# A sparse graph layer on one core: whole 8 KB runs of the matrix, x and out in blocks of four tiles, and new orders of work on three engines

## The chip, the cores and the metric

One core of one Trainium2 chip. The metric is the device time of one execution in microseconds (us); the program runs alone. The core has five engines that run their own instruction streams and meet at semaphores: TensorE (PE), VectorE (DVE), ScalarE (ACT), GpSimd (POOL) and SyncE (SP). SP issues the plain transfers and GpSimd the indirect ones (gathers), each into its own DMA queue; 16 DMA engines serve both.

## The reference

x is 8192 × 512 and adj 8192 × 8192, both in float32. Few entries of adj are positive: about nine in a row, the one on the diagonal always among them. The layer is

```python
h = jnp.maximum(_layernorm(x, axis=-1), 0.0)
mask = adj > 0
head = mask.astype(adj.dtype)
head = head / jnp.maximum(jnp.sqrt(jnp.sum(head * head, axis=-1, keepdims=True)), 1e-12)
inc = adj + head
out = x + (inc @ h) / jnp.sum(inc, axis=-1, keepdims=True)
```

so each positive entry of a row gets a constant added (one over the root of their number), and the product is divided by the row's sum.

## The kernel before, in words

The matrix is not multiplied: its positive entries are found, the rows of h that they name are gathered, and small products add them up.

**Stage 1** (up to about 80 us) reads x in 16 blocks of 1 MB, computes h and stores it in DRAM (`h_scratch`). In a block c, partition p holds the four adjacent rows 512c + 4p + j. The first four blocks (16 tiles of x) stay in SBUF (`held`, x_held).

**Stage 2** runs over 64 tiles of 128 rows. Tile t is c = t // 4, j = t % 4: partition p holds row 512c + 4p + j. SP loads a tile's 4 MB into one of two buffers `A[:, t % 2]` in four chunks of 1 MB (`load_chunk`, L378). Chunk j holds columns 1024j and on of the left half and the same columns of the right half, two runs of 4 KB in each partition:

```python
adj_h = adj.rearrange("(c p j) (h n) -> c j p h n", p=P, j=ROWS, h=2)
sp.dma_start(chunk(t % 2, j), adj_h[t // ROWS, t % ROWS, :, :, CW * j:CW * (j + 1)])
```

VectorE folds the two halves of a chunk into one word per column pair (`fold`, L774), takes the eight largest of each chunk (MAX8, L779) and their places (FIND_INDEX8, L783). That is up to 32 candidates a row, of which 8 are the "own" ones of each row; what is left over goes to "spill" places that rows of a tile share, in three groups of 128. Between the folds VectorE does the small steps of earlier tiles: weights (L914), ranks of the spilled entries (L859) and, after they were brought to their places by TensorE, their entries (L941, own_entry). Tiles 62 and 63 are "wide": unfolded, searched in eight parts (L797, L802), with four spill groups. Rows for which the fold lost an entry go, up to 128 of them, through one extra "batch" tile, number 64, gathered row by row. A dense path for more such rows stands at the end and has no rows here.

The engines are staggered. In period t VectorE searches tile t, and with p = t−1, q = t−2, r = t−3, f = t−4 the others do, each in an order written out by hand:

- **TensorE** (`period`, L1361): find_owner(q), product_spill(f) (L1341, 3 products of 128×128 by 128×512), residual(q) (L1318 adds x, then L1323 adds the row's own h by a diagonal), offsets(p) (L1278), bring_spill(q) (L1301 writes pbrought, L1307 pturned), product_own(q) (L1330, eight products with diagonals). A product leaves two records in the profile. product_spill(f) ends tile f and releases acc_ready.
- **ScalarE** (`period`, L669): check 0 of tile t, own_matrices(q) (L632, nine diagonals), row_again(q) (L642, h of the tile's own rows from x), spill_columns(r) and spill_matrix(r) (L615, L623), roots(p) (L585), copy_owner(q) (L607), checks 1 and 2, finish_tile(f) (L649, copies the sum out of PSUM, waits for acc_ready), reach_places(p) (L593 to L600), check 3. The checks (L569) read the whole tile once more and count its zeros, to find rows that the fold can't take. The buffer of a chunk is loaded again when the fold and the check have read it.
- **GpSimd** (loop at L514): gather_spill(t−2), 3 gathers of 128 rows of h, then gather_own(t), 8 gathers (L488).
- **SP** (loop at L412): chunks 0 and 1 of tile t+2, the store of out of tile t−4 (`store_tile`, L394, from one of two buffers osb, named out_tile), the load of x of tile t from tile 16 on (`load_x`, L387, into one of two buffers xres, named x_residual), chunks 2 and 3 of tile t+2. x and out move 256 KB at a time, 2 KB in a row.

`batch_period` (L701 on ScalarE, L1383 on TensorE) and `drain` (L1399) end the staggered work.

## Time and profile before

| | |
|---|---|
| Runs of the kernel before | 1261.79, 1264.53, 1265.77 us; median 1264.53 |
| The profiled execution's own time | 1265.03 us |
| Its span (first to last instruction) | 1263.2 us |
| VectorE busy | 1162.8 us (92%) |
| ScalarE busy | 977.8 us (77%) |
| TensorE busy | 970.4 us (77%), mean granted clock 0.908 |
| GpSimd busy | 764.9 us (61%) |
| DMA | 471.29 MB, mean 373 GB/s |

How to read it: the busy time of an engine is that of its instructions, without the waits between them; TensorE's products are pipelined, so that its busy share does not mean that each product runs at its peak. In a timeline a line is one instruction or a run of adjacent ones of one kind, with the time that it starts, the time it takes, and in brackets how long its engine idled before it and which event ended that.

### The profile page before, as it was taken

To read this page: it belongs to the slowest core of one execution; us is meant where nothing else is said; L and a number is where in the kernel's file an instruction comes from. 1 tells how busy PE (TensorE), PEld (TensorE's weight loads), DVE (VectorE), ACT (ScalarE), POOL (GpSimd) and SP (SyncE) were. 2 spreads that over 40 slices of the span, in tenths; PEclk is the share of its full clock that TensorE was granted. 3 is DMA by queue.
4 is the path that set the end of the run, shared out by engine and by line. 5 is a ranking of instruction groups with operands and counts; after the bars stand their busy time and mean duration, and the time that the engine had idled before them with its cause. 6 is when DMAs were issued, how large, how long until landed. Compare 5 with 4: busy or idle time off the path is not lost.

```text
span 1263.2 us, 14630 instructions
## 1 busy us (share of the span) xinstructions
PE 970.4 (77%) x2678; PEld 482.8 (38%) x2678; DVE 1162.8 (92%) x2794; ACT 977.8 (77%) x1903; POOL 764.9 (61%) x745
## 2 busy tenths in 40 slices
PE   0002889988888888888888888798888878878676
PEld 0001334444444434444433444344444434434343
DVE  6679999999999999999998999989999989998972
ACT  6657888898888887888887787788878778876551
POOL 1003666766666667676666666775666667667453
PEclk9999999888889999889988988988899889998698
DMA  9999999999999999999999999999999999999442
GB/s 360 428 421 406 398 402 392 392 394 399 396 391 402 401 399 398 384 401 394 384 398 368 400 398 391 388 395 373 402 400 400 385 382 387 398 399 355 142 143 79
DMA packets 148127, 471.29 MB, mean 373 GB/s; under 512 B 24386, under 2 KB 24386, under 8 KB 143876
## 3 DMA queue, kind: packets, MB, share of 16 engines
q1 hardware_dynamic: 90368, 331.38, 66.9%
q0 software_dynamic: 57664, 138.93, 29.9%
q8 instruction: 25, 0.41, 0.1%
q14 instruction: 70, 0.57, 0.1%
HBM read 490.21 MB, written 33.82 MB: 415 GB/s over the span
## 4 chain that ended last, share of the span: by engine, by line
DVE 45%; DMA 20%; issue 20%; ACT 5%; SPq 5%; another core or an unknown queue 2%; PE 1%; DVEq 0%; ACTq 0%; POOL 0%; POOLq 0%
DMA adj_tile<-in_adj_dram 17%; DVE folded L774 15%; DVE cand_word L779 12%; DVE cand_index L783 5%; DMA gathered_rows<-in_x_dram 3%; SPq L385 2%; ACT junk L569 2%; DVE cand_word L797 2%; SPq L392 2%; DVE cand_index L802 2%; ACT adj_tile L556 2%; SPq L396 1%; DVE ln_stats L757 1%; DVE weights_and_payload L914 1%
## 5 line engine op out<-in xcount | busy, mean ns | idle before, releaser
L488 POOL DMA_INDIRECT gathered_rows<-h_scratch,slot_column x520 | 536.8, 1032 | 265.9 <-issue 161.2
L569 ACT ACTIVATE junk<-adj_tile,zero_unit 128x2048 bf16<-128x2048 f32 x256 | 510.1, 1994 | 111.2 <-issue 75.5
L1330 PE MATMUL acc<-gathered_rows,diag 128*128 128x512 f32 x1040 | 504.1, 641 | 0.5 <-issue 0.5
L488 POOL DMA_INDIRECT gathered_rows<-h_scratch,spill_column x197 | 220.5, 1119 | 199.0 <-ACT spill_column L615 150.8
L774 DVE SCALAR_TENSOR_TENSOR folded<-adj_tile 128x1024 f32<-128x1024 f32 x248 | 301.4, 1215 | 12.1 <-DMA adj_tile<-in_adj_dram 10.7
L1330 PEld LDWEIGHTS acc<-gathered_rows,diag 128*128 128x128 f32 x1040 | 213.7, 212 | 247.1 <-issue 246.8
L779 DVE MAX8 cand_word<-folded 128x8 f32<-128x1024 f32 x248 | 302.9, 1221 | 2.2
L783 DVE FIND_INDEX8 cand_index<-cand_word,folded 128x8 uint32<-128x1024 f32 x248 | 302.2, 1218 | 0.0
L1341 PE MATMUL acc<-gathered_rows,spill_matrix 128*128 128x512 f32 x394 | 186.3, 607 | 14.6 <-issue 10.7
L632 ACT ACTIVATE diag<-ident,weights_and_payload 128x128 f32<-128x128 f32 x582 | 176.2, 387 | 0.5 <-DVE weights_and_payload L914 0.5
L1278 PE MATMUL poff<-spill_rank,lanes_before 128*128 128x1 f32 x130 | 26.4, 272 | 187.5 <-DVE spill_rank L859 174.4
L1278 PEld LDWEIGHTS poff<-spill_rank,lanes_before 128*128 128x128 f32 x130 | 25.4, 227 | 239.8 <-issue 139.7
L1341 PEld LDWEIGHTS acc<-gathered_rows,spill_matrix 128*128 128x128 f32 x394 | 73.9, 194 | 103.0 <-issue 102.9
L1323 PE MATMUL acc<-own_row,diag 128*128 128x512 f32 x124 | 75.2, 691 | 45.4 <-ACT own_row L642 29.2
L1307 PE MATMUL pturned<-ident,owner 128*128 128x128 f32 x394 | 79.2, 355 | 0.0
L1301 PE MATMUL pbrought<-weights_and_payload,owner 128*128 128x72 f32 (+1 forms) x386 | 71.4, 333 | 3.5 <-ACT owner L607 3.3
L1307 PEld LDWEIGHTS pturned<-ident,owner 128*128 128x128 f32 x394 | 68.8, 257 | 0.0
L615 ACT ACTIVATE spill_column<-entry 128x3 uint32<-128x3 f32 (+1 forms) x65 | 12.8, 198 | 72.3 <-issue 44.1
L1318 PE MATMUL acc<-x_residual,ident 128*128 128x512 f32 x96 | 53.2, 637 | 17.9 <-issue 14.3
L1301 PEld LDWEIGHTS pbrought<-weights_and_payload,owner 128*128 128x128 f32 x386 | 62.5, 239 | 5.9 <-ACT owner L607 4.5
L623 ACT ACTIVATE spill_matrix<-pturned,entry 128x128 f32<-128x128 f32 x197 | 56.6, 356 | 3.9 <-remote 3.9
L1323 PEld LDWEIGHTS acc<-own_row,diag 128*128 128x128 f32 x124 | 23.1, 211 | 88.1 <-ACT diag L632 46.0
(146 smaller groups left out, 829.8 us busy)
## 6 DMA issues: line engine op xcount, KB each, us to landing
adj_tile<-in_adj_dram SPq DMA_DIRECT2D x256, 1024.0 KB
h_scratch<-adj_tile SPq DMA_DIRECT2D x16, 1024.0 KB, 10.5
out_dram<-out_tile SPq DMA_DIRECT2D x64, 256.0 KB
gathered_rows<-in_x_dram SPq DMA_DIRECT2D x12, 1024.0 KB, 12.6
x_residual<-in_x_dram SPq DMA_DIRECT2D x48, 256.0 KB
gathered_rows<-h_scratch,slot_column POOLq DMA_INDIRECT x520
x_held<-in_x_dram SPq DMA_DIRECT2D x4, 1024.0 KB, 7.9
gathered_rows<-h_scratch,spill_column POOLq DMA_INDIRECT x197
```

The costliest lines, as they stand in the source:

```text
L488: nc.gpsimd.indirect_dma_start(out=into, out_offset=None, in_=h[:, :], in_offset=bass.IndirectOffsetOnAxis(ap=column, axis=0), bounds_chec ...
L569: nc.scalar.activation(junk[:, n % 2].rearrange("p (j c) -> p j c", j=2), both[:, :, half], ACT.Relu, bias=zero_unit[:], scale=-UP, accum_ ...
L623: last = nc.scalar.activation(W[:, t % 2, g], pturned[:, g * P:(g + 1) * P], ACT.Copy, scale=entry[:, t % 2, g, 0:1])
L632: last = nc.scalar.activation(diag[:, t % 2, s], ident[:], ACT.Copy, scale=wpay[:, t % 2, s:s + 1])
L774: nc.vector.scalar_tensor_tensor(out=F[:, j % 2], in0=a[:, 1], scalar=UP, in1=a[:, 0], op0=ALU.mult, op1=ALU.add).then_inc(folded, 1)
L779: nc.vector.max(out=cv[:, t % 2, 8 * j:8 * j + 8], in_=F[:, j % 2]).then_inc(vals_found, 1)
L783: nc.vector.max_index(out=ci[:, t % 2, 8 * j:8 * j + 8], in_max=cv[:, t % 2, 8 * j:8 * j + 8], in_values=F[:, j % 2]).then_inc(idx_found, 1)
L1301: last = nc.tensor.matmul(bank[:, c:c + 3 * n], owner[:, g * P:(g + 1) * P], wpay[:, t % 2, 1 + OWN:1 + OWN + 3 * n], start=True, stop=True)
L1307: last = nc.tensor.matmul(pturned[:, g * P:(g + 1) * P], owner[:, g * P:(g + 1) * P], ident[:], start=True, stop=True)
L1323: nc.tensor.matmul(acc[t % 3][:], diag[:, t % 2, 0], again[:], start=False, stop=False).then_inc(row_added, 1)
L1330: last = nc.tensor.matmul(acc[t % 3][:], diag[:, t % 2, 1 + s], slot(t % 2, s), start=False, stop=False)
L1341: last = nc.tensor.matmul(acc[t % 3][:], W[:, t % 2, g], slot(t % 2, OWN + g), start=False, stop=(g == groups(t) - 1))
```

## The change

Four things change together.

1. **Runs of the matrix.** A chunk is 2048 adjacent columns, one run of 8 KB in each partition. The fold joins the chunk's own two halves, so columns n and n + 1024 instead of n and n + 4096; constants of columns, the place of the diagonal and the numbering of the wide tiles' parts follow.
2. **x and out.** Five blocks of x (20 tiles) are held instead of four; out of a tile is written by finish_tile over its x in the same place. SP stores out in 16 blocks of 1 MB (8 KB runs) and loads the other 11 blocks of x as 1 MB where a block has been stored. The small buffers and the semaphore res_added go away; finish_tile no longer waits for a store.
3. **Orders.** GpSimd gathers own rows of tile t ahead of the spill rows of t−2; the gather of x for the batch tile goes behind the loop. TensorE does residual and product_own first, then offsets, bring_spill, and product_spill(f) last. ScalarE does row_again(q) and own_matrices(q) ahead of check 0, moves roots behind check 1, and does finish_tile(f) last, behind check 3.
4. **Batch tile.** It gets four spill groups like the wide tiles, and one VectorE step of the final marking goes away.

The diff, cut to its core:

```diff
-    HELD_CHUNKS = 4
+    HELD_CHUNKS = 5
...
-    x_t = x.rearrange("(c p j) d -> c j p d", p=P, j=ROWS)
-    out_t = out.rearrange("(c p j) d -> c j p d", p=P, j=ROWS)
-    adj_h = adj.rearrange("(c p j) (h n) -> c j p h n", p=P, j=ROWS, h=2)
+    out_ln = out.rearrange("(c p j) d -> c p j d", p=P, j=ROWS)
+    adj_t = adj.rearrange("(c p j) n -> c j p n", p=P, j=ROWS)
...
-            return EXTRA if FOLDED <= t < BATCH else FOLDED_EXTRA
+            return EXTRA if wide(t) else FOLDED_EXTRA
...
-                sp.dma_start(chunk(t % 2, j), adj_h[t // ROWS, t % ROWS, :, :, CW * j:CW * (j + 1)]).then_inc(adj_loaded[t % 2][j], 16)
-
-            def load_x(t):
-                if t >= HELD + 2:
-                    sp.wait_ge(res_added, t - 1)
-                    if not wide(t - 2):
-                        sp.wait_ge(row_ready, t - 1)
-                sp.dma_start(xres[:, t % 2], x_t[t // ROWS, t % ROWS]).then_inc(x_loaded[t % 2], 16)
-
-            def store_tile(t):
-                sp.wait_ge(out_ready, t + 1)
-                sp.dma_start(out_t[t // ROWS, t % ROWS], osb[:, t % 2]).then_inc(out_stored[t % 2], 16)
+                sp.dma_start(A[:, t % 2, 2 * CW * j:2 * CW * (j + 1)],
+                             adj_t[t // ROWS, t % ROWS, :, 2 * CW * j:2 * CW * (j + 1)]).then_inc(adj_loaded[t % 2][j], 16)
+
+            def load_x(c):
+                sp.wait_ge(out_stored[(c - HELD_CHUNKS) % 2], 16 * ((c - HELD_CHUNKS) // 2 + 1))
+                sp.dma_start(group(c), x_ln[c]).then_inc(x_loaded[c % 2], 16)
+
+            def store_group(c):
+                sp.wait_ge(out_ready, ROWS * c + ROWS)
+                sp.dma_start(out_ln[c], group(c)).then_inc(out_stored[c % 2], 16)
...
-                if t >= 4:
-                    store_tile(t - 4)
-                if t >= HELD:
-                    load_x(t)
+                if t >= 2 * ROWS and t % ROWS == 0:
+                    store_group(t // ROWS - 2)
+                if t % ROWS == 2 and HELD_CHUNKS <= t // ROWS - 2 + HELD_CHUNKS < LN:
+                    load_x(t // ROWS - 2 + HELD_CHUNKS)
...
-                gather_spill(t - 2)
-                if t < BATCH:
-                    gather_own(t)
+                gather_own(t)
+                if t >= 2:
+                    gather_spill(t - 2)
...
             def finish_tile(t):
                 act.wait_ge(acc_ready, t + 1)
-                if t >= 2:
-                    act.wait_ge(out_stored[t % 2], 16 * (t // 2))
-                nc.scalar.activation(osb[:, t % 2], acc[t % 3][:], ACT.Copy).then_inc(out_ready, 1)
+                nc.scalar.activation(out_of(t), acc[t % 3][:], ACT.Copy).then_inc(out_ready, 1)
...
-                check(t, 0)
                 if pay:
-                    own_matrices(q)
                     if not wide(q):
                         row_again(q)
+                    own_matrices(q)
...
+                check(t, 0)
                 if pick:
                     spill_columns(r)
                     spill_matrix(r)
-                if small:
-                    roots(p)
                 if pay:
                     copy_owner(q)
                 check(t, 1)
+                if small:
+                    roots(p)
                 check(t, 2)
-                if end:
-                    finish_tile(f)
                 if small:
                     reach_places(p)
                 check(t, 3)
+                if end:
+                    finish_tile(f)
...
                 if pay:
                     find_owner(q)
-                if end:
-                    product_spill(f)
...
                 if pay:
                     residual(q)
+                    product_own(q, 0)
+                    product_own(q, 1)
                 offsets(p)
                 if pay:
                     bring_spill(q)
-                    product_own(q, 0)
-                if pay:
-                    product_own(q, 1)
+                if end:
+                    product_spill(f)
...
                 step(nc.vector.scalar_tensor_tensor(out=w_well[:, 6], in0=end_all[:, last],
                                                     scalar=float(PLACES), in1=w_well[:, 5], op0=ALU.is_le, op1=ALU.add))
-                step(nc.vector.scalar_tensor_tensor(out=w_well[:, 6, TILES - FOLDED:], in0=end_all[:, BATCH:BATCH + 1],
...
```

In `batch_period` the same two moves are made: on TensorE product_spill(u) goes behind product_own of the next tile but two, on ScalarE finish_tile(u) goes behind the first check of the batch tile.

## Rows read from the trace of the kernel before

**Rows 1.** The page: busy time of the engines, DMA share in 40 slices, gather queue.

```profile
PE 970.4 (77%) x2678; PEld 482.8 (38%) x2678; DVE 1162.8 (92%) x2794; ACT 977.8 (77%) x1903; POOL 764.9 (61%) x745
...
DMA  9999999999999999999999999999999999999442
...
q0 software_dynamic: 57664, 138.93, 29.9%
```

**Rows 2.** Windows: stretch, length, PE, PEld, DVE, ACT, POOL busy, PEclk, DMA share, GB/s.

```profile
150.00:430.00 280.00, 244.08 (x690) 123.34 (x689) 277.98 (x652) 236.60 (x465) 190.81 (x185) 0.91 1.02 396
430.00:1126.00 696.00, 596.85 (x1645) 294.52 (x1644) 665.93 (x1561) 568.51 (x1119) 471.18 (x441) 0.91 1.02 392
```

**Rows 3.** VectorE's timeline: the first fold of tiles 1, 36, 37 and 61.

```profile
97.81 1.22 DVE L774 SCALAR_TENSOR_TENSOR folded<-adj_tile 128x1024 f32<-128x1024 f32 x1 [1.18 <-DMA adj_tile<-in_adj_dram]
...
692.87 1.22 DVE L774 SCALAR_TENSOR_TENSOR folded<-adj_tile 128x1024 f32<-128x1024 f32 x1
...
709.56 1.22 DVE L774 SCALAR_TENSOR_TENSOR folded<-adj_tile 128x1024 f32<-128x1024 f32 x1
...
1126.32 1.21 DVE L774 SCALAR_TENSOR_TENSOR folded<-adj_tile 128x1024 f32<-128x1024 f32 x1
```

**Rows 4.** DMA view, 31.6 to 50 us, then 90 to 105 us: packets, MB, share.

```profile
q1 hardware_dynamic: 1086, 7.86, 101.0%
...
q1 hardware_dynamic: 1497, 6.26, 102.4%
```

**Rows 5.** ScalarE's timeline around 661, 693 and 705 us.

```profile
661.25 0.80 ACT L642 ACTIVATE own_row<-x_residual,ln_bias,ln_rstd 128x512 f32<-128x512 f32 x1
661.96 0.19 ACT L615 ACTIVATE spill_column<-entry 128x3 uint32<-128x3 f32 x1
...
693.36 2.73 ACT L632 ACTIVATE diag<-ident,weights_and_payload 128x128 f32<-128x128 f32 x9
...
704.89 0.57 ACT L649 ACTIVATE out_tile<-acc 128x512 f32<-128x512 f32 x1
705.37 0.16 ACT L593 ACTIVATE half_minus_offset<-poff 128x1 f32<-128x1 f32 x1
```

**Rows 6.** TensorE's timeline around 664, 702 and 1251 us.

```profile
663.98 1.02 PE L1323 MATMUL acc<-own_row,diag 128*128 128x512 f32 x2
664.84 0.28 PE L1278 MATMUL poff<-spill_rank,lanes_before 128*128 128x1 f32 x2
...
666.40 7.03 PE L1330 MATMUL acc<-gathered_rows,diag 128*128 128x512 f32 x16
...
701.62 0.38 PE L1278 MATMUL poff<-spill_rank,lanes_before 128*128 128x1 f32 x2 [1.85 <-DVE spill_rank L859]
701.86 0.87 PE L1301 MATMUL pbrought<-weights_and_payload,owner 128*128 128x72 f32 x6
...
703.28 8.73 PE L1330 MATMUL acc<-gathered_rows,diag 128*128 128x512 f32 x16
...
1251.11 2.74 PE L1341 MATMUL acc<-gathered_rows,spill_matrix 128*128 128x512 f32 x6
```

**Rows 7.** Windows: the stretches around these own products, columns as in rows 2.

```profile
660.00:674.00 14.00, 13.79 (x45) 6.89 (x44) 13.40 (x31) 9.44 (x21) 10.82 (x11) 1.00 1.03 399
703.30:706.70 3.40, 3.40 (x7) 1.34 (x6) 3.37 (x5) 3.40 (x7) 2.65 (x3) 0.50 1.03 400
```

**Rows 8.** VectorE's timeline: own_entry, then the first searches of both wide tiles.

```profile
712.47 0.22 DVE L941 TENSOR_TENSOR own_entry<-pbrought,place_plus_half 128x72 f32<-128x72 f32 x1
...
1143.68 1.22 DVE L797 MAX8 cand_word<-adj_tile 128x8 f32<-128x1024 f32 x1
...
1169.48 1.21 DVE L797 MAX8 cand_word<-adj_tile 128x8 f32<-128x1024 f32 x1
```

**Rows 9.** DMA view, 263 to 268 us: both queues, packets, MB, share.

```profile
q1 hardware_dynamic: 338, 1.15, 59.3%
q0 software_dynamic: 291, 0.80, 41.9%
```

More of the change, by code:

```diff
@@ L190, in x_of, with group, out_of, x_come @@
         def x_of(t):
-            return held[:, t] if t < HELD else xres[:, t % 2]
-        def x_turn(t):
-            return (t - HELD) // 2 + 1
+            return held[:, t % HELD]
+        def group(c):
+            k = c % HELD_CHUNKS
+            return held[:, ROWS * k:ROWS * (k + 1), :]
+        def out_of(t):
+            return again[:] if t == BATCH else held[:, t % HELD]
+        def x_come(t):
+            c = t // ROWS
+            return x_loaded[c % 2], 16 * ((c - HELD_CHUNKS) // 2 + 1)
         incT = F[:, 0, 0:2 * P].rearrange("p (b c) -> p b c", b=2)
@@ L242, in searched @@
             return CHUNKS * min(t, FOLDED) + PARTS * max(t - FOLDED, 0)
-        def part(i):
-            return i % 2 * CHUNKS + i // 2
         def paid(t, k):
@@ L422, in _ @@
                     load_chunk(t + 2, 3)
-            for t in range(TILES - 4, TILES):
-                store_tile(t)
+            for c in range(LN - 2, LN):
+                store_group(c)
             for b in range(2):
-                sp.wait_ge(out_stored[b], 16 * (TILES // 2))
+                sp.wait_ge(out_stored[b], 16 * (LN // 2))
             sp.wait_ge(list_ready, 1)
@@ L434, in _ @@
                     sp.dma_start(A[:, 0, :], adj[bass.ds(row, P, step=ROWS), :]).then_inc(d_adj, 16)
-                    sp.dma_start(xres[:, 0], x[bass.ds(row, P, step=ROWS), :]).then_inc(d_x, 16)
+                    sp.dma_start(held[:, 0], x[bass.ds(row, P, step=ROWS), :]).then_inc(d_x, 16)
                     for c in range(NCH):
@@ L440, in _ @@
                     sp.wait_ge(d_out, j + 1)
-                    sp.dma_start(out[bass.ds(row, P, step=ROWS), :], osb[:, 0]).then_inc(d_stored, 16)
+                    sp.dma_start(out[bass.ds(row, P, step=ROWS), :], held[:, 1]).then_inc(d_stored, 16)
                     sp.wait_ge(d_stored, j * 16 + 16)
@@ L511, in _ @@
                 pool.wait_ge(h_stored[b], 16 * (LN // 4))
-            gather_own(0)
-            gather_own(1)
-            for t in range(2, BATCH + 1):
+            for t in range(BATCH - 1):
                 if t == BATCH - 2:
@@ L704, in batch_period @@
                 own_matrices(w)
-                finish_tile(u)
                 check_batch(0)
@@ L708, in batch_period @@
                 reach_places(y)
+                finish_tile(u)
                 check_batch(1)
@@ L786, in part_columns @@
             def part_columns(t, i):
-                if t == BATCH:
-                    return A[:, 0, CW * part(i):CW * (part(i) + 1)]
-                return chunk(t % 2, part(i) % CHUNKS)[:, part(i) // CHUNKS]
+                return A[:, t % 2, CW * i:CW * (i + 1)]
             def part_values(t, i):
@@ L794, in part_values @@
                 else:
-                    dve.wait_ge(adj_loaded[t % 2][part(i) % CHUNKS], 16 * turn(t))
-                e = slice(8 * part(i), 8 * part(i) + 8)
+                    dve.wait_ge(adj_loaded[t % 2][i // 2], 16 * turn(t))
+                e = slice(8 * i, 8 * i + 8)
                 nc.vector.max(out=cv[:, t % 2, e], in_=part_columns(t, i)).then_inc(vals_found, 1)
@@ L800, in part_places @@
                 dve.wait_ge(vals_found, searched(t) + i + 1)
-                e = slice(8 * part(i), 8 * part(i) + 8)
+                e = slice(8 * i, 8 * i + 8)
                 nc.vector.max_index(out=ci[:, t % 2, e], in_max=cv[:, t % 2, e],
@@ L1316, in residual @@
                 elif t >= HELD:
-                    pe.wait_ge(x_loaded[t % 2], 16 * x_turn(t))
-                nc.tensor.matmul(acc[t % 3][:], ident[:], again[:] if t == BATCH else x_of(t), start=True,
-                                 stop=False).then_inc(res_added, 1)
+                    pe.wait_ge(*x_come(t))
+                nc.tensor.matmul(acc[t % 3][:], ident[:], again[:] if t == BATCH else x_of(t), start=True, stop=False)
                 if not wide(t):
@@ L1385, in batch_period @@
                 find_owner(w)
-                product_spill(u)
                 residual(w)
@@ L1391, in batch_period @@
                 product_own(w, 1)
+                product_spill(u)
                 find_owner(y)
```

41 lines of the change are left out of this document (19 added, 22 removed).

## The prediction

> **What bounds the kernel now.** I read the page first. Its busy line and slices [rows 1] show VectorE busy for 92% of the span, TensorE for 77%, and the DMA engines full until the last three slices. Two limits thus lie close together, and the windows by stage [rows 2] separate them only a little: from 150 to 430 us VectorE is busy 277.98 of 280 us, from 430 to 1126 us 665.93 of 696, while the DMA share is 1.02 in both. The starts of the first fold of a tile [rows 3] give the pitch: (1126.32 − 97.81)/60 = 17.14 us a tile, where an undelayed tile takes 709.56 − 692.87 = 16.69. So the loop costs 60 × 0.45 = 27 us over what VectorE needs. The other side of the same number is the traffic: 16.69 us at 392 GB/s move 6.54 MB, and a tile needs 4.19 MB of the matrix, 138.93/65 = 2.14 MB of gathered rows [rows 1] and 0.46 MB of x and out, 6.79 MB or 17.3 us. VectorE is the floor at 16.7 and the DMA engines hold the loop 0.4 above it. ScalarE and TensorE have slack, and this change spends it.
>
> **The change part by part.**
>
> *Matrix in 8 KB runs.* Before, a chunk is two 4 KB runs a partition. No row shows 8 KB runs of the matrix, but the loads of x at the start are 8 KB runs with nothing beside them, and 90 to 105 us is almost only matrix [rows 4]: 7.86 MB in 18.4 us, 427 GB/s, against 6.26 MB in 15.0 us, 417. 64 tiles of 4.19 MB are 268.4 MB: 643.6 − 628.6 = 15 us less DMA time. The bounds are 0 (the two stretches differ in direction too, since the first holds stores of h) and, with the shares of 102.4% and 101.0% counted in, 268.4 × (1.024 × 15.0/6.26 − 1.01 × 18.4/7.86) = 24 us. I take 15, the time that passed.
>
> *x and out in blocks.* 48 + 64 transfers of 256 KB in 2 KB runs become 11 + 16 of 1 MB in 8 KB runs: 29.4 MB. The gathers are 2 KB rows; their queue moved 138.93 MB in 29.9% of 1263.2 us [rows 1], 368 GB/s. At that rate 29.4 MB take 79.9 us, at 427 GB/s 68.9: 11 us less. Bounds 0 and, if stores lose as much again by short runs, 22. SP issues fewer transfers, and load_x and store_group stand where load_x and store_tile stood, ahead of chunks 2 and 3 of tile t+2. The store at turn t waits for out_ready of tile t−5, finished at the end of period t−1, the load for a store issued two turns before; I cost both waits at nothing, because a 1 MB transfer takes some 3 us at 400 GB/s and they have two turns of 17 us. Without that cover each late one would hold two chunks back, once in four tiles. The sum of both DMA parts is 26 us, 0.41 a tile of 64: 17.14 becomes 16.73, no longer above VectorE's 16.69.
>
> *The orders of TensorE and ScalarE.* Here the path changes. Before, product_spill(f) is second in TensorE's period and finish_tile(f) comes after check 2 on ScalarE: it never waits in the loop, and the diagonals and the row of tile q lie between checks. After, product_spill(f) is the last of TensorE's period, finish_tile(f) is ScalarE's last and waits for it, and the next period's row_again and nine diagonals stand behind it; TensorE's row product and own products wait for those diagonals, and offsets, bring_spill and product_spill stand behind them. That closes a ring of one turn per tile through both engines, worked out from ScalarE's rows [rows 5] and TensorE's rows at full clock [rows 6]:
> - finish_tile until the next instruction: 705.37 − 704.89 = 0.48.
> - row_again 661.96 − 661.25 = 0.71, nine diagonals 2.73.
> - the row product 664.84 − 663.98 = 0.86.
> - the eight own products 7.03 (16 records).
> - offsets, pbrought and pturned: 666.40 − 664.84 = 1.56.
> - product_spill 2.74 for three groups.
>
> This is 16.11; with the handovers between the engines I take 16.2 us. What else ScalarE does (checks, spill_matrix, copy_owner, roots, reach_places) lies beside TensorE's 12.2 us: its busy 568.51 of 696 us [rows 2] are 14.0 a tile, less 3.9 in the ring 10.1. Against 16.7 the ring would be just hidden, if TensorE stayed at full clock.
>
> *The clock.* In each turn TensorE has nothing but find_owner and the residual to do while ScalarE does 0.48 + 0.71 + 2.73 = 3.92 us: it idles about 3 us (3.92 less one product of 0.86). Before, a wait of 1.85 us ahead of offsets [rows 6] was followed by a stretch at granted clock 0.50, the 1.2 GHz level [rows 7], and the own products took 8.73 us there, against 7.03 in the stretch at 1.00: 1.70 us lost. The new idle is longer and stands straight ahead of the same products. With one such stretch a turn the ring takes 16.2 + 1.7 = 17.9 us. The lower bound is the loop's own mean clock, 0.91 [rows 2]: TensorE's 12.19 us become 13.4, and the ring 17.4. The upper bound is a second such stretch in a third of the turns, 17.9 + 0.57 = 18.5. I take 17.9, since the row with the idle ahead is nearest to what the ring makes.
>
> *What of it the end sees.* 60 × (17.9 − 17.14) = +45.6. Some of the lag is hidden. own_entry on VectorE starts at 712.47 [rows 8], 9.7 us after pbrought came (701.86 + 0.87) [rows 6]; bringing it behind the own products uses about 7 of these and leaves some 3 at the beginning of the loop. At the end the wide tiles take VectorE 1169.48 − 1143.68 = 25.8 us each [rows 8], so that a ring of 17.9 regains perhaps half of 7.9. Together −7, an estimate (bounds 0 and −12).
>
> *Small parts.* GpSimd issues the own gathers of t ahead of the spill gathers of t−2: own rows come three issues earlier, spill rows eight later, and by the code both are used a period or more after their issue; nothing on the path. The gather of x for the batch tile stands behind the loop, ahead of tile 61's spill gathers, and is used later still: nothing. The batch tile gets a fourth group: a third of 2.74 on TensorE, 0.9, and about 0.5 for one more matrix and gather: +1.4, an estimate, in the tail, where nothing covers it; the marking step removed on VectorE is within its rounding. finish_tile loses its wait for a store and TensorE its release of x, both met long before; nothing. The last store is 1 MB in place of 256 KB: 0 to +4 us, but it lies beside the batch tile's work (product_spill of its predecessor ends at 1253.85 [rows 6]): 0.
>
> **Sum** against the profiled execution's 1265.0: +45.6 − 7 + 1.4 = +40, thus 1305; the median of the runs shown is 0.5 lower, 1304.5. The DMA relief does not appear in it, since the ring, not the transfers, sets the pitch. Its own range is 1275 (17.4) to 1339 (18.5).
>
> **Rivals.**
> - *The ring stays hidden (faster).* TensorE keeps its clock, as in the stretch at 1.00 [rows 7], and the pitch falls to 16.73: 60 × −0.41 + 1.4 = −23, 1241. For it: 16.2 is below 16.7 at full clock, and the DMA engines do lose 26 us of work. Against it: the clock was 0.91 with less idle than the ring makes, and the ring has 0.5 us to lose. It decides where less than 0.5 us of TensorE's clock is lost per turn.
> - *The two cancel (same).* Half of the turns have such a stretch: 16.2 + 0.85 = 17.05; 60 × −0.09 + 1.4 = −4, 1260.5; with a little more of it 1268.
> - *Gathers starve (slower).* In 5 us with both queues busy [rows 9] the loads send 338 packets of 140 ns and the gathers 291 of 115 ns: nearly turn by turn. With the loads' packets twice as long the gathers' share falls from 0.41 to 115/395 = 0.29, and their 5.8 us a tile (29.9% of 1263.2 over 65) take 20 us instead of 14. They would then set 20 us for as long as loads always queue; as loads stop when both buffers are full, I count between a sixth and a half of the excess of 2.9 over 17.14: 60 × 0.5 = +30 to 60 × 1.4 = +85, 1294 to 1350, about 1323 for a third. For it: packets do grow with the runs (1086 for 7.86 MB of 8 KB runs, 1497 for 6.26 MB of 4 KB runs) [rows 4]. Against it: the rows' lead of a period. The Trainium skill, "DMA: Bandwidth & Descriptors", section "Queues, rings and completion order", states the rule behind this: an engine takes turns between the queues at packet granularity. The near equality of 338 and 291 agrees with it; by it alone the longer packet takes time from the gathers.
> - *8 KB runs are no faster.* Then DMA still needs 17.14, and with the ring hidden the time is that of before.
>
> **How the numbers follow.** The forecast 0.56, starved gathers 0.08, cancelling or no faster packets 0.12, hidden ring 0.24. A measurement of this kernel tells 0.3%, 3.8 us, from no change. Slower is 0.56 + 0.08, the same 0.12, faster 0.24. The range reaches from the hidden ring's own centre, 1241, which leaves out half of it (0.12), to 1340, which leaves out the worst of starving and of the clock (0.08).
>
> **What would show it.** Right: ScalarE's finish_tile waits for product_spill in most tiles, by a few us; TensorE's largest idle is ahead of the row product, released by the diagonals; the slices' clock is below before's; the DMA share falls under 1 within the loop; first folds 17.4 to 18.5 apart, VectorE waiting for checked buffers or pbrought. Wrong: folds 16.7 apart with VectorE full and finish_tile hardly waiting (the hidden ring), or TensorE waiting for gathered rows (starved gathers). Right about the DMA part but wrong about the sign would be a stretch of loads at over 420 GB/s and a ring near 16.5.

## The result and the profile after

The changed kernel takes 1394.56 us (median of 4 runs, 1389.9 to 1397.09), the kernel before 1264.97: ratio 1.1025, 95% interval 1.099 to 1.1061. It is slower, as forecast, but by 130 us, not 40, and outside the range. Two of the four executions of e9 below fell in the chip's slower state (1378.3 and 1386.6 us) and are left out of its median. The profiled execution took 1389.9 us, its span 1388.2, 125.0 more than before.

The page of the changed kernel: busy time, slices of VectorE, granted clock and DMA, and the chain that ended last, by engine (those of before are [rows 1]).

```profile
PE 1022.1 (74%) x2684; PEld 475.7 (34%) x2684; DVE 1171.9 (84%) x2795; ACT 975.5 (70%) x1904; POOL 788.7 (57%) x746
...
DVE  6689988899788988888888898898899888887972
...
PEclk9999888899888889888888888888888888888889
DMA  9999988999999899999999999999999989988443
...
PE 46%; ACT 21%; issue 14%; another core or an unknown queue 6%; DMA 6%; DVE 5%; POOL 0%; ACTq 0%; SPq 0%; POOLq 0%; DVEq 0%
```

No engine is full now. VectorE fell from 92% to 84%, and the chain that ended last lies for two thirds on TensorE and ScalarE. The windows of the same stretches as [rows 2], same columns:

```profile
150.00:430.00 280.00, 226.05 (x592) 104.25 (x590) 246.51 (x576) 210.85 (x416) 180.48 (x163) 0.87 0.94 352
430.00:1126.00 696.00, 565.81 (x1483) 261.60 (x1482) 605.71 (x1408) 511.08 (x1010) 435.61 (x399) 0.86 0.94 355
```

The DMA share went from 1.02 to 0.94 and the granted clock from 0.91 to 0.86: the transfers wait for the engines. VectorE's timeline, the first fold of tiles 1 and 61, to be held against [rows 3]:

```profile
97.59 1.23 DVE L772 SCALAR_TENSOR_TENSOR folded<-adj_tile 128x1024 f32<-128x1024 f32 x1 [1.09 <-DMA adj_tile<-in_adj_dram]
...
1242.53 1.22 DVE L772 SCALAR_TENSOR_TENSOR folded<-adj_tile 128x1024 f32<-128x1024 f32 x1
```

The pitch is (1242.53 − 97.59)/60 = 19.08 us a tile, 1.94 more than before: 116.4 us. From the first fold of tile 61 to the end it takes 1388.2 − 1242.53 = 145.7 us, before 136.9: another 8.8. Both together are the difference of the spans, but for 0.2 us ahead of tile 1.

Two turns of the ring, on ScalarE's timeline (finish_tile is L647, reach_places L593) and on TensorE's (row product L1315, own products L1322, product_spill L1333):

```profile
712.55 0.60 ACT L647 ACTIVATE x_then_out<-acc 128x512 f32<-128x512 f32 x1 [1.22 <-PE acc L1333]
713.05 0.80 ACT L642 ACTIVATE own_row<-x_then_out,ln_bias,ln_rstd 128x512 f32<-128x512 f32 x1
713.75 2.72 ACT L632 ACTIVATE diag<-ident,weights_and_payload 128x128 f32<-128x128 f32 x9
...
726.37 0.17 ACT L593 ACTIVATE half_minus_offset<-poff 128x1 f32<-128x1 f32 x1 [2.43 <-PE poff L1271]
...
732.57 0.60 ACT L647 ACTIVATE x_then_out<-acc 128x512 f32<-128x512 f32 x1 [3.40 <-remote]
...
750.80 0.60 ACT L647 ACTIVATE x_then_out<-acc 128x512 f32<-128x512 f32 x1 [1.22 <-issue]
```

```profile
716.53 1.76 PE L1315 MATMUL acc<-own_row,diag 128*128 128x512 f32 x2 [2.20 <-ACT diag L632]
718.08 8.14 PE L1322 MATMUL acc<-gathered_rows,diag 128*128 128x512 f32 x16
726.05 0.28 PE L1271 MATMUL poff<-spill_rank,lanes_before 128*128 128x1 f32 x2
...
727.61 2.74 PE L1333 MATMUL acc<-gathered_rows,spill_matrix 128*128 128x512 f32 x6
...
736.54 2.08 PE L1315 MATMUL acc<-own_row,diag 128*128 128x512 f32 x2 [1.94 <-ACT diag L632]
738.41 8.21 PE L1322 MATMUL acc<-gathered_rows,diag 128*128 128x512 f32 x16
746.46 0.28 PE L1271 MATMUL poff<-spill_rank,lanes_before 128*128 128x1 f32 x2
...
748.02 2.74 PE L1333 MATMUL acc<-gathered_rows,spill_matrix 128*128 128x512 f32 x6
```

From one finish_tile to the next: 716.53 − 712.55 = 3.98 on ScalarE (forecast 3.92), row product 1.55 (0.86), own products 7.97 (7.03), offsets to pturned 1.56 (1.56), and from the start of product_spill to finish_tile 732.57 − 727.61 = 4.96 (2.74): 20.02 us. The next turn ends at 750.80, after 18.23 us, with 1.87, 8.05 and 2.78 in the same places. The ring is the one forecast, step by step; every ScalarE step has its forecast length, the row product and the own products are longer in both turns, and in the first turn finish_tile starts 2.2 us after the end that the profile models for product_spill ("remote": the profile finds no event that ended the wait; "issue": the engine waited for nothing that it shows). Means of the same steps over the 55 turns between 160 and 1240 us: 3.98, 1.77, 8.11, 1.58 and 3.77, together 19.21.

### The profile page after: what moved, and what is told of

Its sections match the earlier page's. It is cut to its first block, busy times and chain, and to the rows that moved or that the text cites. A ratio compares the mean times of both kernels' runs of the same rounds, so it can differ in the third digit from the quotient of the medians.

```text
span 1388.2 us, 14444 instructions
## 1 busy us (share of the span) xinstructions
PE 1022.1 (74%) x2684; PEld 475.7 (34%) x2684; DVE 1171.9 (84%) x2795; ACT 975.5 (70%) x1904; POOL 788.7 (57%) x746
## 4 chain that ended last, share of the span: by engine, by line
PE 46%; ACT 21%; issue 14%; another core or an unknown queue 6%; DMA 6%; DVE 5%; POOL 0%; ACTq 0%; SPq 0%; POOLq 0%; DVEq 0%
PE acc L1322 29%; ACT diag L632 9%; ACT junk L569 8%; PE acc L1315 7%; PE acc L1333 6%; DMA gathered_rows<-in_x_dram 3%; ACT adj_tile L556 1%; PE pbrought L1294 1%; DMA gathered_rows<-h_scratch,slot_column 1%; PE pturned L1300 1%; ACT from_first_place L600 1%; DMA adj_tile<-in_adj_dram 1%; DVE folded L772 1%; ACT own_row L642 1%
## 5 line engine op out<-in xcount | busy, mean ns | idle before, releaser
L487 POOL DMA_INDIRECT gathered_rows<-h_scratch,slot_column x520 | 564.2, 1085 | 496.0 <-DVE slot_column L877 351.6
L1322 PE MATMUL acc<-gathered_rows,diag 128*128 128x512 f32 x1040 | 537.0, 675 | 3.1 <-DMA gathered_rows<-h_scratch,slot_column 3.1
L1322 PEld LDWEIGHTS acc<-gathered_rows,diag 128*128 128x128 f32 x1040 | 235.6, 227 | 331.9 <-issue 331.8
L1315 PE MATMUL acc<-own_row,diag 128*128 128x512 f32 x124 | 122.3, 1087 | 131.3 <-ACT diag L632 122.5
L1333 PE MATMUL acc<-gathered_rows,spill_matrix 128*128 128x512 f32 x396 | 183.7, 600 | 2.7 <-DMA gathered_rows<-h_scratch,spill_column 2.7
L1311 PE MATMUL acc<-x_then_out,ident 128*128 128x512 f32 x128 | 83.4, 738 | 91.6 <-ACT x_then_out L647 63.0
L593 ACT ACTIVATE half_minus_offset<-poff 128x1 f32<-128x1 f32 x65 | 11.1, 171 | 192.3 <-PE poff L1271 110.3
L647 ACT ACTIVATE x_then_out<-acc 128x512 f32<-128x512 f32 x64 | 38.2, 596 | 134.0 <-remote 75.9
L889 DVE RECIPROCAL head<-root 128x1 f32<-128x1 f32 x65 | 10.5, 162 | 126.9 <-ACT root L585 85.0
L1315 PEld LDWEIGHTS acc<-own_row,diag 128*128 128x128 f32 x124 | 28.9, 289 | 192.4 <-ACT diag L632 179.2
L1333 PEld LDWEIGHTS acc<-gathered_rows,spill_matrix 128*128 128x128 f32 x396 | 71.2, 193 | 68.9 <-issue 66.2
L1311 PEld LDWEIGHTS acc<-x_then_out,ident 128*128 128x128 f32 x128 | 21.2, 205 | 130.2 <-ACT x_then_out L647 84.6
L1294 PE MATMUL pbrought<-weights_and_payload,owner 128*128 128x72 f32 (+1 forms) x384 | 57.0, 285 | 7.9 <-DVE weights_and_payload L915 7.1
L1300 PE MATMUL pturned<-ident,owner 128*128 128x128 f32 x396 | 58.5, 285 | 0.0
```

What stands on the lines that cost most here:

```text
L487: nc.gpsimd.indirect_dma_start(out=into, out_offset=None, in_=h[:, :], in_offset=bass.IndirectOffsetOnAxis(ap=column, axis=0), bounds_chec ...
L1294: last = nc.tensor.matmul(bank[:, c:c + 3 * n], owner[:, g * P:(g + 1) * P], wpay[:, t % 2, 1 + OWN:1 + OWN + 3 * n], start=True, stop=True)
L1300: last = nc.tensor.matmul(pturned[:, g * P:(g + 1) * P], owner[:, g * P:(g + 1) * P], ident[:], start=True, stop=True)
L1311: nc.tensor.matmul(acc[t % 3][:], ident[:], again[:] if t == BATCH else x_of(t), start=True, stop=False)
L1315: nc.tensor.matmul(acc[t % 3][:], diag[:, t % 2, 0], again[:], start=False, stop=False).then_inc(row_added, 1)
L1322: last = nc.tensor.matmul(acc[t % 3][:], diag[:, t % 2, 1 + s], slot(t % 2, s), start=False, stop=False)
```

## The experiments

Sixteen kernels, in the order in which they were run. A new expectation rests on what came before it. Medians, and ratios to the kernel before with their 95% intervals:

| Run | What it is | us | Ratio |
|---|---|---|---|
| e1 | changed, old orders on ScalarE and TensorE | 1444.7 | 1.1442 [1.1408, 1.1476] |
| e2 | changed, product_spill second | 1557.4 | 1.2311 [1.227, 1.2352] |
| e3 | changed, offsets early | 1413.2 | 1.12 [1.1166, 1.1234] |
| e4 | before, new orders on ScalarE and TensorE | 1565.8 | 1.2388 [1.2362, 1.2414] |
| e5 | changed, finish late, offsets early | 1292.6 | 1.0243 [1.0225, 1.0262] |
| e6 | changed, all old orders | 1273.6 | 1.0074 [1.0047, 1.01] |
| e7 | changed, finish late | 1313.9 | 1.0398 [1.0369, 1.0426] |
| e8 | changed, GpSimd's old order | 1553.8 | 1.2302 [1.228, 1.2325] |
| e9 | changed, two added products a tile | 1350.7 | none, two runs: 1346.6 and 1354.8 us |
| e10 | e5, two added products a tile | 1284.3 | 1.0193 [1.0163, 1.0223] |
| e11 | before, 8 KB runs, three groups | 1780.2 | 1.41 [1.4074, 1.4125] |
| e12 | before, blocks of x and out | 1266.6 | 1.0051 [1.003, 1.0072] |
| e13 | before, 8 KB runs, four groups | 1270.1 | 1.0064 [1.004, 1.0088] |
| e14 | changed, fourth sum, finish a period later | 1274.7 | 1.0107 [1.0069, 1.0145] |
| e15 | e14 with 4 KB runs | 1267.4 | 1.0033 [1.0012, 1.0054] |
| e16 | e14, own products behind bring_spill | 1264.8 | 1.002 [1.0, 1.0039] |

**The orders belong together (e1 to e4, e8).** The first set undid one part of the orders each.

The diffs of this section are cut to the lines that carry each change. In e1 the part of the change in period and batch_period of ScalarE and TensorE is taken back, in e4 that part alone is made in the kernel before. On TensorE, e1 against the changed kernel:

```diff
                     find_owner(q)
+                if end:
+                    product_spill(f)
...
                     residual(q)
-                    product_own(q, 0)
-                    product_own(q, 1)
                 offsets(p)
                 if pay:
                     bring_spill(q)
+                    product_own(q, 0)
+                if pay:
+                    product_own(q, 1)
-                if end:
-                    product_spill(f)
```

e2 is the move of product_spill alone, e3 the move of offsets alone:

```diff
                     residual(q)
-                    product_own(q, 0)
-                    product_own(q, 1)
                 offsets(p)
                 if pay:
+                    product_own(q, 0)
+                    product_own(q, 1)
                     bring_spill(q)
```

> The changed kernel with ScalarE's and TensorE's orders of before in period and batch_period; 8 KB runs, blocks of x and out, GpSimd's new order stay. Ring theory (finish_tile last on ScalarE behind product_spill last on TensorE, with the diagonals of the next tile behind it): the ring is gone, the pitch falls from 19.1 to about 16.7 us a tile, the time to about 1241 us, below before. Rival, the data movement (8 KB packets or blocks of x starve the gathers or stall the loads): stays above 1330.

> The changed kernel with product_spill(f) alone moved back to second place in TensorE's period. Ring theory: finish_tile no longer waits; what is left is a shorter ring (row_again and diagonals 3.4, row product 0.9, own products 7.0, offsets 0.1, reach_places 0.7, check 3 2.0, finish_tile 0.5: 14.6 us, with 1.7 to 2.7 of lost clock 16.3 to 17.3), so 1240 to 1280 us. Rival (offsets behind the own products, for which ScalarE's reach_places waits 192 us in all, is what costs): that wait stays, so the time stays above 1350.

> The changed kernel with offsets(p) alone moved ahead of the own products on TensorE, as before the change; product_spill(f) stays last. Ring theory: ScalarE's wait ahead of reach_places goes, and the same time is waited ahead of finish_tile; the ring has lost nothing: 1380 to 1400 us. Rival (the wait for offsets is what costs): faster by most of 192 us less what lies beside other work, below 1320.

> The kernel before with only ScalarE's and TensorE's new orders; 4 KB runs, x and out of 256 KB, GpSimd's old order stay. Ring theory: the ring sets the pitch whatever the transfers do, so 1380 to 1400 us as in the changed kernel. Rival (data movement): about 1265, as before. If both matter, between.

e1 and e2 fell far on the wrong side: by their orders the ring through product_spill and finish_tile was cut, and the kernels got slower still. e4 came out at 1566, beyond both theories. The waits of e1 and e4 (engine, line, releaser: us in all, times, longest) point to why:

```profile
PE acc L1333 <- DMA gathered_rows<-h_scratch,spill_column: 329.3, 36, 15.4
```

```profile
POOL gathered_rows L488 <- ACT spill_column L615: 475.3, 63, 8.6
...
ACT out_tile L649 <- remote: 315.8, 59, 6.3
DVE head L893 <- ACT root L585: 309.9, 58, 8.4
```

In e1 GpSimd issues the spill rows behind eight own gathers, and TensorE wants them second in its period: it stands 329 us for them. In e4 GpSimd stands 475 us (150.8 before) for spill_columns before it may issue the own rows, and TensorE now wants those first. e8 gives the changed kernel GpSimd's old order alone:

```diff
-                gather_own(t)
-                if t >= 2:
-                    gather_spill(t - 2)
+                gather_spill(t - 2)
+                if t < BATCH:
+                    gather_own(t)
```

> The changed kernel with GpSimd's order of before alone (spill rows first). Theory, from the run of the kernel before with the new orders of two engines: GpSimd stands waiting for spill_columns before it may issue the own rows, which TensorE now wants first; so slower than the changed kernel, near 1560 us, whatever the runs of the matrix. Rival (GpSimd's order is neutral): 1394.

The gather of x for the batch tile goes back into the loop as well. 1553.8, as expected from e4. So "own first" on GpSimd and product_spill last on TensorE are one step; either without the other gave kernels of 1445 to 1566 us. e1 and e2 therefore say nothing of the ring. e3 does: with offsets early the wait ahead of reach_places goes and the kernel gains nothing (1413, even above the 1380 to 1400 expected). What waited 192 us there waits ahead of finish_tile instead, 152.4 + 142.6 + 34.4 us against 40.5 + 75.9 + 17.6 in the changed kernel.

**Cutting the ring (e5, e7).** Here finish_tile copies a tile one period later, so that product_spill is out of the way of the next diagonals:

```diff
-                p, q, r, f = t - 1, t - 2, t - 3, t - 4
+                p, q, r, f = t - 1, t - 2, t - 3, t - 5
...
                     own_matrices(q)
+                if end:
+                    finish_tile(f)
...
                 check(t, 3)
-                if end:
-                    finish_tile(f)
```

> The changed kernel with finish_tile one period later only; offsets stay behind the own products. Ring theory: product_spill is out of the ring, but residual, row and own products, offsets, reach_places, check 3, row_again, diagonals and finish_tile still make one of 15.4 us at full clock, 17 to 18 with the clock it loses: 1260 to 1330 us, between the changed kernel and the one with offsets early as well. Rival (the place of finish_tile costs nothing): 1394.

> The changed kernel, GpSimd's new order and product_spill last kept, with both chains through ScalarE cut: finish_tile copies a tile one period later, behind the diagonals, and offsets(p) stands ahead of the own products. Ring theory: TensorE needs 13.5 us a turn and waits only for finish_tile (0.5), so VectorE and the transfers bound again: pitch 16.7 to 16.9, 1240 to 1255 us. Rival (8 KB runs and blocks, or own rows first on GpSimd, cost by themselves): above 1330.

Moving one copy of half a microsecond takes 81 us away (1313.9): the place of finish_tile is the cause, and the shorter ring through offsets and reach_places is left as expected. Cutting that as well (e5 has the move of e3 too) gives 1292.6, neither the 1240 to 1255 of the theory nor the rival's 1330.

**The data half (e6, e11 to e13).** e6 puts all three orders back. e12 and e13 split its two halves. e11 lacked the fourth group of the batch tile.

With the rest of the constants for adjacent columns, e13 is this in the kernel before, and e11 the same without the last pair of lines:

```diff
-adj_h = adj.rearrange("(c p j) (h n) -> c j p h n", p=P, j=ROWS, h=2)
+adj_t = adj.rearrange("(c p j) n -> c j p n", p=P, j=ROWS)
-            return EXTRA if FOLDED <= t < BATCH else FOLDED_EXTRA
+            return EXTRA if wide(t) else FOLDED_EXTRA
```

e12 takes the other half: 20 held tiles, out over x, and load_x and store_group:

```diff
-    HELD_CHUNKS = 4
+    HELD_CHUNKS = 5
...
-                    store_tile(t - 4)
...
-                    load_x(t)
+                if t >= 2 * ROWS and t % ROWS == 0:
+                    store_group(t // ROWS - 2)
```

> The changed kernel with the orders of before on GpSimd, ScalarE and TensorE; only the 8 KB runs, the blocks of x and out and the fourth group stay. Theory (the orders belong together, and the transfers are a gain of about 0.4 us a tile): about 1241 us, 1236 to 1255. Rival (longer packets starve the gathers, or x and out in blocks hold up the loads): above 1270.

> The kernel before with the 8 KB runs of the matrix alone; x and out stay at 256 KB, all orders of before. Theory from the run with all old orders (packets of twice the length leave the gathers 103/(103+292) = 0.26 of the DMA engines while loads queue, and they need 0.32): own and spill products wait for gathered rows, 1266 to 1282 us, the loads' gain is lost. Rival (the blocks of x and out are what spoils it): 1245 to 1257.

> The kernel before with the blocks of x and out alone (held 20 tiles, out over x, 1 MB each); the matrix stays in 4 KB runs, all orders of before. Theory (long packets of the matrix starve the gathers, blocks are a small gain, 5 to 11 us of DMA work): 1252 to 1262. Rival (the blocks hold up loads or gathers): 1270 to 1285, and runs alone a gain.

> The kernel before with the 8 KB runs of the matrix and the batch tile's fourth group; x and out at 256 KB, all orders of before. The run without the fourth group went through the dense path five times, so its time says nothing of the runs; its loop took 17.12 us a tile, as before (17.14). Theory (the loads' gain is lost because the gathers wait for longer packets): 1262 to 1274 us, TensorE waiting for gathered rows as it did not before. Rival (blocks of x and out spoilt the run with all old orders): 1240 to 1255.

e11 ran the dense path five times (its profile counts five of the dense path's roots), so the fourth group is no small part: the new fold needs it, at least with these inputs. Neither half is a gain: blocks 1.005, runs 1.006, both 1.007 (e6, 1273.6, where its theory said 1236 to 1255). The waits of e13 for transfers:

```profile
PE acc L1322 <- DMA gathered_rows<-h_scratch,slot_column: 45.0, 24, 4.0
PE acc L1333 <- DMA gathered_rows<-h_scratch,spill_column: 39.8, 21, 4.2
...
ACT junk L566 <- DMA adj_tile<-in_adj_dram: 10.9, 3, 6.0
...
DVE folded L771 <- DMA adj_tile<-in_adj_dram: 4.2, 4, 1.3
```

In the kernel before, TensorE waited 3.9 us for spill rows and hardly for own rows, and ScalarE and VectorE 34.6 and 10.7 us for the matrix. With 8 KB runs the matrix is in time and the gathered rows are late; that this is what takes e13's gain away is inferred from these waits. The rivals that wanted a gain from one half fell; so did the small gain that was expected of the blocks. Why e12 is half a per cent slower is not settled.

**The clock (e9, e10).** Two products that nobody reads fill TensorE's idle:

```diff
+            def keep_busy(t):
+                if t < FOLDED - 1:
+                    for _ in range(2):
+                        nc.tensor.matmul(ptr[0][:], ident[:], placeno[:], start=True, stop=True)
...
+                keep_busy(t)
                 if not wide(t):
                     pe.wait_ge(diag_ready, t + 1)
```

> The changed kernel with two more 128x512 products by the identity on TensorE in each folded tile, between residual and the row product, into a bank of PSUM that nothing reads then: work that is added and used by nobody. Theory (the ring of 16.2 us at full clock is stretched to 19.1 by the clock that TensorE loses after its idle ahead of the row product): the idle is filled, the clock stays near 1.00, the pitch falls towards 16.7 to 17.2: 1245 to 1285 us. Rival (the ring is that long for another reason, the handovers or the waits for DMA): no gain, or up to 1.7 us a tile more, 1394 to 1500.

> The version with finish_tile one period later and offsets early, with the same two added products a tile, here behind find_owner. There finish_tile still waits for product_spill in two tiles of three and every third tile takes 19.1 us. If lost clock stretches product_spill: the pitch becomes 16.7, 1240 to 1255 us, below the kernel before. If not (gathers or VectorE's waits): 1290 to 1310.

More work made the kernel faster: 1350.7, between the theory and its rival. In the profiled execution (1346.6) the mean granted clock was 0.949, against 0.871, and the pitch 18.34. Where the clock stayed at 1.00 and nothing else was late the ring took what the prediction said for full clock, 16.2 us:

```profile
700.87 0.60 ACT L647 ACTIVATE x_then_out<-acc 128x512 f32<-128x512 f32 x1 [1.22 <-PE acc L1340]
...
717.23 0.60 ACT L647 ACTIVATE x_then_out<-acc 128x512 f32<-128x512 f32 x1 [1.43 <-PE acc L1340]
```

```profile
704.85 1.12 PE L1322 MATMUL acc<-own_row,diag 128*128 128x512 f32 x2 [0.49 <-ACT diag L632]
705.81 7.03 PE L1329 MATMUL acc<-gathered_rows,diag 128*128 128x512 f32 x16
```

That is 16.36 us; 14 of 55 turns are between 16.1 and 16.4. On the mean the row product and the own products together fell from 9.88 to 8.45 us a turn, though half of that came back in other places: from product_spill to finish_tile it took 4.17 in place of 3.77, ahead of the row product 4.33 in place of 3.98. So the clock is a part of the loss, 0.7 us of the turn in that execution, but not all. e10 has the same products behind find_owner in e5:

```diff
                     find_owner(q)
+                    keep_busy(q)
```

It gained 8 us, little more than the second theory of its expectation allowed. Its clock was 0.972 and finish_tile still waited 129 us for releases of TensorE that come later than the profile's modelled ends; 13 of 60 tiles still took 19 us or more (15 in e5).

**Cutting it for good (e14 to e16).** offsets share a bank of PSUM with the owners, behind copy_owner; the free bank becomes a fourth sum, and finish_tile stands behind check 1, a period after product_spill (offsets also move between the own products, and roots ahead of copy_owner):

```diff
-        acc = [... for b in range(3)]
-        poff = ctx.enter_context(nc.psum_tensor("poff", [P, 512], fp32))
+        acc = [... for b in range(4)]
+        poff = powner
...
-                if t >= 3:
-                    pe.wait_ge(out_ready, t - 2)
+                if t >= 4:
+                    pe.wait_ge(out_ready, t - 3)
...
                 check(t, 1)
+                if end:
+                    finish_tile(f)
```

> The changed kernel with the ring cut for good: a fourth sum in PSUM (offsets share the bank of the owners, behind copy_owner), so that finish_tile may copy a tile a whole period after product_spill, behind check 1, and nothing waits for it; offsets between the own products, roots ahead of copy_owner; 8 KB runs, blocks and GpSimd's new order stay. Theory (the ring and late releases of acc_ready through it are all that is left of the changed kernel's loss): pitch 16.7 to 17.0, 1237 to 1258 us, below before. Rival (own rows first, or starved gathers, cost by themselves): 1275 to 1295, as with finish_tile one period later.

> The same schedule (fourth sum, finish_tile behind check 1 a period later, own rows first) with the matrix in 4 KB runs as before the change. If long packets starve the gathers even in this schedule: faster than the one with 8 KB runs, 1240 to 1255. If the 8 KB runs are a gain once the schedule has slack: slower by 5 to 20 us than it.

e15 is the same edit, with GpSimd's new order and the orders of e14, on e12 (so the batch tile has three spill groups). With the ring gone 120 of the 130 us are gone (1274.7), though not all: the theory's 1237 to 1258 was missed and the rival's 1275 nearly met. 4 KB runs gain 7 more (1267.4) and not the 20 of the expectation. What is left is in the waits of e14, and of e15 with 4 KB runs:

```profile
PE acc L1324 <- DMA gathered_rows<-h_scratch,slot_column: 145.9, 73, 4.2
```

```profile
ACT junk L572 <- DMA adj_tile<-in_adj_dram: 89.1, 35, 5.8
PE acc L1332 <- DMA gathered_rows<-h_scratch,slot_column: 27.4, 37, 2.2
DVE folded L776 <- DMA adj_tile<-in_adj_dram: 26.7, 35, 2.4
```

The same trade as between e13 and before: long packets delay gathers, short ones the matrix. The DMA view of e14, 300 to 305 us (packets, MB, share), shows how:

```profile
q1 hardware_dynamic: 190, 1.34, 68.7%
q0 software_dynamic: 189, 0.51, 26.5%
```

Turn for turn, but a load's packet now takes 0.687 × 80/190 = 0.29 us of an engine and a gather's 0.11, so that the gathers get 0.27 of the engines where they need 0.33 on the average of the loop. By the rule of the Trainium skill, "DMA: Bandwidth & Descriptors", section "Queues, rings and completion order" (an engine takes turns between queues packet by packet), that is what longer packets do; in this stretch the trace agrees, 190 to 189. In others the loads paused and the gathers caught up: from 310 to 315 us the loads sent 124 packets and the gathers 456, in 59.0% of the engines.

e16 moves the own products behind bring_spill, to give their rows time, and on ScalarE copy_owner behind check 0:

```diff
-                    product_own(q, 0)
                 offsets(p)
                 if pay:
-                    product_own(q, 1)
                     bring_spill(q)
+                    product_own(q, 0)
+                    product_own(q, 1)
```

> The version with the fourth sum and 8 KB runs, where TensorE waited 146 us in all for own rows that had not landed; here the own products stand behind bring_spill on TensorE (product_spill still last), and copy_owner straight behind check 0 so that bring_spill is not late. Theory (what keeps the cut ring above the kernel before is only the gathers' lateness behind long packets, about 2 us each): own products start 3 to 5 us later, find their rows, TensorE has a period's slack for it: pitch 16.8 to 17.1, 1245 to 1263 us. Rival (another wait takes its place, releases or the DMA engines' total): 1268 to 1280, as with the own products first.

1264.8, 2 us above the theory's range and 10 us below e14; TensorE's wait for own rows fell from 145.9 to 41.6 us. So the rows' lateness was what e14 had left over. It equals the kernel before (1.002) and doesn't beat it. No version here does.

## Why the prediction was wrong in size

- **The ring: right.** Its place, its order and its ScalarE terms are in the timelines above, its 16.2 us at full clock are in e9, and cutting it (e7, e14) takes back 81 and 120 us. "finish_tile waits by a few us" held: 134 us in all, in 60 of the 64 tiles. VectorE's sign did not: it waited neither for checked buffers nor for pbrought but mostly for roots on ScalarE, ahead of head (126.9 us).
- **The step that failed: "with the handovers between the engines I take 16.2 us".** It gives all handovers 0.09 us a turn, from no row. From product_spill's start to finish_tile a turn took 3.77 us on the mean of 55 turns, where product_spill itself takes 2.74: 1.0 us. In 27 of the turns finish_tile starts 0.03 us behind the modelled end, in 28 it is 0.4 to 5.0 us later, 2.2 in the first turn above. finish_tile's waits that the profile calls "remote" are 75.9 us. In a ring every late release moves all that follows. What delays a release isn't settled.
- **The clock's term: right in kind, a little small.** "One such stretch a turn" held: in 53 of the 55 turns a part of the row product and the own products ran at 1.2 GHz, and the row product and the own products took 9.88 us in place of 7.89: 2.0 lost, where 1.7 were forecast. The bound by the mean clock of before was no bound, for in the loop the granted clock was 0.86 to 0.87: TensorE's 12.19 us at 0.865 are 14.1, which gives a ring of 18.1. With the 1.0 us of late releases that is the 19.1 measured.
- **The hidden lag: wrong sign.** The step "−7" counted on VectorE's slack at both ends of the loop. The tail became 8.8 us longer instead: 1.8 in tile 61, 2.5 in the two wide tiles, 3.3 in the batch tile's searches and 1.2 behind them. The step also rested on a misread row: the search at 1169.48 [rows 8] is the seventh of tile 62, and tile 63 starts in

```profile
1174.39 1.21 DVE L797 MAX8 cand_word<-adj_tile 128x8 f32<-128x1024 f32 x1
```

so the wide tiles took 30.7 and 23.8 us before, not 25.8 each, and there was more room than the prediction thought, yet nothing was regained there. (The product_spill that ends at 1253.85 is the batch tile's own, not its predecessor's; that term was put at nothing and changes no sum.) In the profiled executions the miss is 125 − 40 = 85 us: 60 × (19.08 − 17.9) = 71 for the turn, and 8.8 in place of −7, less the fourth group's 1.4, which lies in that tail and which no run measures by itself. The median lies another 4.7 above the profiled execution.
- **The hidden ring's 1241: not to be had.** The DMA work did fall: from 430 to 1126 us the two queues took, before and in e14 (packets, MB, share):

```profile
q1 hardware_dynamic: 54903, 188.24, 69.6%
q0 software_dynamic: 35214, 84.06, 32.4%
```

```profile
q1 hardware_dynamic: 25625, 186.61, 67.2%
q0 software_dynamic: 35377, 84.05, 32.6%
```

That is 1.020 × 696/272.3 = 2.61 us a MB before and 0.998 × 696/270.7 = 2.57 in e14, 1.6%, or 0.3 us a tile against the 0.41 forecast. But e6, e13 and e14 are not 0.3 us a tile faster: for e14 the runs show late gathers as the price (e15, e16), for e6 and e13 only their waits do. Nor was all of the 0.45 us over VectorE's 16.69 the transfers': half of it lies in three tiles of another kind, which the last section shows. The rival "gathers starve" was right as a mechanism, and "with a period's lead" was the wrong reason to set it aside: the lead is there in the order of the code, but own rows used first in TensorE's period were late 73 times in e14. Its price is small, at most 7 us (e14 to e15) to 10 us (e14 to e16), not the 30 to 85 of the prediction; the loads do pause and let the gathers catch up, as between 310 and 315 us.
- **GpSimd's order at nothing: right only in company.** In the change as made TensorE waits 5.8 us in all for gathered rows at its products; e1, e2, e4 and e8 show that this holds because product_spill went last at the same time.

## What to carry to other kernels

Where an order is written by hand for several engines, follow each release around until it comes back to the engine that it started from: a copy of 0.5 us at the end of one engine's period, waiting for the last product of another, tied two loops into one turn and cost 81 to 120 us, and a buffer more with a copy a period later took it back. Weigh such a ring with the TensorE clock that its own idle leaves and with releases that come late, as other rows of the same trace show them, not with full-clock rows and one correction; a margin of 0.5 in 16.7 us is none. Longer transfers on one queue are not free for short ones on another: look at who waits for which transfer before and after, not at the DMA share alone.

## What the runs showed of the hardware that was not expected

Releases of TensorE came much later than the ends that the profile models, at a granted clock of 1.00. The kernel before has such a stretch too, on TensorE's and VectorE's timelines:

```profile
664.98 0.87 PE L1301 MATMUL pbrought<-weights_and_payload,owner 128*128 128x72 f32 x6
```

```profile
679.09 0.23 DVE L941 TENSOR_TENSOR own_entry<-pbrought,place_plus_half 128x72 f32<-128x72 f32 x1 [4.35 <-remote]
```

own_entry waits for nothing but that product by its code, and waited 4.35 us, until 679.09, where the product's modelled end is 665.85; that tile took 21.7 us. From 660 to 674 us the granted clock was 1.00 [rows 7], and so it was from 674 to 678. The kernel before has three such tiles, of 21.7, 21.8 and 21.8 us, with waits of 4.35, 5.01 and 3.62 us at own_entry. They hold 15 of the 27 us that its loop takes over VectorE's 16.69 a tile, 13 of them in these waits; the prediction put all 27 down to the transfers. Whether TensorE itself ran behind the modelled times or only its signal was late isn't shown by any run.

The second thing: adding two useless products a tile made a kernel 44 us faster (1394.6 to 1350.7), with the granted clock at 0.949 in place of 0.871: the engine that got more work kept its clock.
